# An attention step's fp32 products in two groups instead of three, tiles and scores alternating

## What is computed

```python
def _L0_attn_ref(hidden_states, Wq, Wkv, Wo):
    ...
    q = (hidden_states @ Wq).reshape(b, s, NUM_HEADS, HEAD_DIM)
    kv = hidden_states @ Wkv
    k, v = (kv[..., :HEAD_DIM], kv[..., HEAD_DIM:])
    scores = jnp.einsum('bqhd,bkd->bhqk', q, k) * scale
    bias = slopes[:, None, None] * (pos[None, None, :] - pos[None, :, None]).astype(jnp.float32)
    scores = jnp.where(causal[None, None], scores + bias[None], -jnp.inf)
    attn = jax.nn.softmax(scores, axis=-1)
    out = jnp.einsum('bhqk,bkd->bqhd', attn, v).reshape(b, s, h)
    return out @ Wo
...
x = x + _L0_attn_ref(_layernorm(x, axis=-1), Wq, Wkv, Wo)
x = x + _L0_ffn_ref(_layernorm(x, axis=-1), qweight, weight_scale, weight_zero_point, bias)
```

## Time and profile before

| | |
|---|---|
| median of three runs | 821.62 us (820.59 to 821.73) |
| the profiled execution | 822.31 us |
| its span, first to last instruction | 820.5 us |
| TensorE busy | 806.4 us (98%) |
| VectorE busy | 594.7 us (72%) |
| GpSimd busy | 429.4 us (52%) |
| ScalarE busy | 372.5 us (45%) |
| mean granted TensorE clock | 0.999 |

### The profile page before, as it was taken

The page is one execution under the profiler, slowest core; times in us unless marked ns, Lnnn a source line. Parts: engine busy times, 40 slices in busy tenths (PEclk is TensorE's granted clock), DMA queues, the critical chain, the costliest instruction groups (busy, mean ns, idle before and its releaser), DMA issues.

```text
span 820.5 us, 13647 instructions
## 1 busy us (share of the span) xinstructions
PE 806.4 (98%) x4618; PEld 583.2 (71%) x4618; DVE 594.7 (72%) x1589; ACT 372.5 (45%) x730; POOL 429.4 (52%) x313
## 2 busy tenths in 40 slices
PE   7999999999999999999999999999999999999997
PEld 5777878888665655556555555688887888888886
DVE  3877554577878889988888896255647779684877
ACT  1755536232466677676666665221401231051322
POOL 1000000000299998899889988522746298363566
PEclk9999999999999999999999999999999999999999
DMA  8867687467566655676566655462064613500012
GB/s 313 315 199 209 229 256 256 154 177 223 152 140 150 152 132 146 146 160 143 134 146 172 156 122 172 151 180 89 1 224 136 198 60 111 194 28 1 38 65 103
DMA packets 71390, 125.85 MB, mean 153 GB/s; under 512 B 7460, under 2 KB 16708, under 8 KB 71240
## 3 DMA queue, kind: packets, MB, share of 16 engines
q1 hardware_dynamic: 71312, 124.97, 52.5%
q10 hardware_dynamic: 8, 0.01, 0.0%
HBM read 85.61 MB, written 38.94 MB: 152 GB/s over the span
## 4 chain that ended last, share of the span: by engine, by line
PE 77%; DMA 7%; DVE 6%; issue 4%; ACT 4%; POOL 1%; SPq 0%; DVEq 0%; POOLq 0%; ACTq 0%
PE p_s L870 11%; PE p_st L899 9%; PE p_o L910 9%; PE p_s L978 5%; PE p_s L980 5%; PE p_s L979 5%; PE p_o L923 5%; PE p_o L809 4%; DMA inv_b<-inv_d 3%; PE p_s L809 2%; PE p_st L978 2%; PE p_st L980 2%; PE p_st L979 2%; PE p_s L1003 2%; PE p_s L1002 2%
## 5 line engine op out<-in xcount | busy, mean ns | idle before, releaser
L1452 DVE CUSTOM_DVE_ANT_0 spill<-p_s,mask 128x128 bf16<-128x128 f32 (+3 forms) x512 | 219.6, 483 | 38.3 <-PE p_s L870 37.6
L1169 ACT ACTIVATE pt<-p_st 128x512 f32<-128x512 f32 (+1 forms) x352 | 178.2, 562 | 101.1 <-PE p_st L899 100.9
L635 POOL TENSOR_SCALAR_AFFINE_SELECT pt<-pt 128x512 f32<-128x512 f32 x128 | 87.5, 696 | 238.7 <-ACT pt L1169 238.7
L870 PE MATMUL p_s<-kst,xt 98*128 98x128 f32 (+3 forms) x512 | 151.1, 343 | 0.9 <-DVE mx L1452 0.7
L899 PE MATMUL p_st<-xt,kst 100*128 100x512 f32 (+1 forms) x352 | 129.4, 387 | 0.7 <-DMA xt<-ml 0.3
L870 PEld LDWEIGHTS p_s<-kst,xt 98*128 98x128 f32 x512 | 91.4, 189 | 52.7 <-DVE mx L1452 42.7
L642 POOL TENSOR_TENSOR pt<-pt 128x1536 f32<-128x1536 f32 x32 | 111.8, 3492 | 2.7
L910 PE MATMUL p_o<-pt,vst 128*32 128x512 f32 (+3 forms) x1024 | 82.4, 439 | 0.0
L648 POOL TENSOR_TENSOR pt<-pt 128x1024 f32<-128x1024 f32 x32 | 76.7, 2396 | 0.0
L899 PEld LDWEIGHTS p_st<-xt,kst 100*128 100x128 f32 x352 | 64.5, 190 | 14.1 <-issue 5.6
L809 PE MATMUL p_o<-xt,wqh 128*128 128x512 f32 x136 | 53.1, 400 | 0.8 <-DVE xt L1603 0.8
(11 more groups left out here) (205 smaller groups left out, 1648.0 us busy)
## 6 DMA issues: line engine op xcount, KB each, us to landing
xt<-qh_d SPq DMA_DIRECT2D x64, 256.0 KB
xs<-in_x_t_dram SPq DMA_DIRECT2D x32, 256.0 KB, 6.2
qh_d<-qh SPq DMA_DIRECT2D x32, 256.0 KB, 3.2
ql_d<-ql SPq DMA_DIRECT2D x32, 256.0 KB, 4.1
xt<-ql_d SPq DMA_DIRECT2D x32, 256.0 KB
o_d<-o_st SPq DMA_DIRECT2D x32, 256.0 KB, 2.3
ob<-o_d SPq DMA_DIRECT2D x32, 256.0 KB, 5.5
xin<-in_x_dram SPq DMA_DIRECT2D x14, 512.0 KB, 7.8
```

The costliest lines, as they stand in the source:

```text
L635: pool.affine_select(out=own, in_=own, compare_op=ALU.is_ge, fill=0.0, base=0, pattern=[[0, 4], [1, P]], channel_multiplier=-1).then_inc(c ...
L870: pe.matmul(scores_of(n), qst[s % 4][0:R_MAX, j, qb * P:(qb + 1) * P], kst[0:R_MAX, b * S:b * S + keys], start=True, stop=True).then_inc(s ...
L1169: act.activation(pt[s % 2][:, j:j + heads, PT_AT[kb]:PT_AT[kb] + KB_LEN[kb]], p_st[:, place(k) % 3, 0:heads * KB_LEN[kb]].rearrange("p (j ...
L1452: dve.tensor_tensor_reduce(spill[:, SPILL_AT[qb]:SPILL_AT[qb] + keys], scores_of(n), mask[:, S - keys:S], 1.0, LOWEST, ALU.add, ALU.max, m ...
```

## The change

It rewrites the two tables of TensorE's order; the other engines' programs, the last step's groups behind the loop and `FIRST_AT` stay as they are.

```diff
-            ORDER = "xuxuxTGxuxuxuxuGuxuxxuuxGxu"
-
-            GROUP = (((0,), ()), ((1, 2, 3), ()), ((), (0, 1)))
+            ORDER = "xuxuxTGuxuxuxuxuxGuxuxuxux"
+
+            GROUP = (((0, 1), ()), ((2, 3), (0, 1)))
```

## The result

The changed kernel takes 840.61 us (median of 4 runs, 839.59 to 841.57) against 821.54 for the kernel before, a ratio of 1.0234 with a 95% interval of 1.0217 to 1.0252. It is slower by 19.1 us. The forecast was 841.9, with +20.3.

A forecast was written before the change was run, and what follows sets the result against it. TensorE was taken to bound the kernel before, at 9.38 us a step. The change's terms sum to +20.3 on the 820.5 us span; the profiled 822.31 becomes 842.6, and the median, 0.69 lower, 841.9 us, range 835 to 851.

The forecast's parts named there:

- U7 of step 1: Start of step 1's eighth score unit, after the wait for step 0's second add: 231.16 instead of 229.78, +1.38 us.
- 28 periods: Steps from U7 of step 1 to U7 of step 29: 28 x 10.15 against 263.89, +20.31 us.
- step 30: Period where VectorE's subtractions hold up GpSimd's cuts: 11.03 against 10.68, +0.35 us.
- step 31: Period that the output projection's first tiles fill on TensorE, longer than the ring: -0.30 us.
- behind U7 of step 31: After the last step's U7, step 30's sums and their entry and exit no longer stand: -1.40 us.
- The group saved: One fp32 group fewer per step on TensorE: 0.30 us saved, its own period from 9.38 to 9.08.
- The ring: Loop from U7 through GpSimd's second add and the sums back to U7: 10.15 us against TensorE's 9.08.
- The handoff: From GpSimd's second add's end to TensorE's sums: 0.14 us, bounds 0.05 to 0.30.
- It will idle 1.07 us in front of the sums.: TensorE, needing 9.08 us alone, waits 1.07 us for GpSimd's second add each step; the step grows 0.73 to 0.77.
- The rival with VectorE falling behind: In the steps, VectorE or the maxima's way falls behind the 1.07 us slack: 0.3 us each, 851; chance 0.06.
- The rival in which the ring does not bind: In the steps, only the group is saved: 821.6 - 9.3 = 812.3 us; chance 0.06.
- VectorE and GpSimd's port: VectorE's subtraction costs nothing; rival: some 26 get in front of an add, 0.6 us each, 858; chance 0.04.

The follow-up runs named there:

- with VectorE relieved and no ring: Changed kernel with its second group moved behind U9 and the maxima taken over the last 128 keys alone: 811.95 us.
- those with three: Kernel before the change, with the maxima taken over the last 128 keys alone: 816.79 us.
- longer by the values: Changed kernel with the sums put in front of the values of blocks 2 and 3 inside the second group: 858.25 us.
- with the ring shortened: Changed kernel with GpSimd's cuts of key blocks 2 and 3 over 8 columns of each head instead of 128: 835.21 us.
- The same order with short maxima: Changed kernel with the sums as a third group directly behind U7 and maxima over the last 128 keys alone: 842.72 us.
- The version with small cuts and short maxima: Changed kernel with cuts of blocks 2 and 3 over 8 columns of each head and maxima over the last 128 keys alone: 827.67 us.
- the changed kernel with short maxima: Changed kernel with VectorE's maxima over the last 128 keys alone instead of up to 512: 839.95 us.

## Why the prediction was right, and where it was not

| step of the forecast | forecast | measured |
|---|---|---|
| ring: U7 to the second add's end | 8.80 | 8.78 |
| ring: GpSimd's end to the sums | 0.14 | 0.06 |
| ring: the sums | 1.21 | 1.21 |
| U7 of step 1 | +1.38 | 230.86 - 229.78 = +1.08 |
| 28 periods | +20.31 | 283.82 - 263.89 = +19.93 |
| step 30 | +0.35 | 11.01 - 10.68 = +0.33 |
| step 31 | -0.30 | 12.41 - 13.17 = -0.76 |
| behind U7 of step 31 | -1.40 | (839.8 - 538.1) - (820.5 - 517.52) = -1.28 |
| sum | +20.3 | +19.3 of the span |

*The group saved.* Right in size: with VectorE relieved and no ring, the plain steps with two groups run at 8.95 us where those with three run at 9.27 (0.32, for a forecast of 0.30). That is the order with the second group behind U9, and over the 28 periods, late steps included, the two differ by only 0.13 (9.18 and 9.31). In the changed kernel none of it is seen.

*The ring.* Right, and shown from both sides: longer by the values (+0.65), longer by a GpSimd operation (+0.58), shortened or cut and the plain step falls.

*The handoff.* The term was 0.08 too long, some 2 us over the kernel. Other bounds added nearly as much: 283.82 is 2.4 more than 28 x 10.05, from the steps with reciprocals and from single steps, above all two (10.89, 10.62) in which TensorE waited for a transfer, 0.81 us for queries and 0.59 for maxima. So the agreement within 1.3 us owes something to two errors of opposite sign.

*"It will idle 1.07 us in front of the sums."* Wrong: 0.18 in a plain step, nothing in those with reciprocals. This part of the forecast's mechanism failed, and with it "TensorE's own period falls from 9.38 to 9.08" as what is left under the ring and, on VectorE, "so I take nothing here"; ScalarE's chain was not looked at. TensorE's path from U7 to the sums depends on both: with the ring shortened it takes 9.83 (10.12 with reciprocals), 9.67 when VectorE is relieved, 9.70 in the steps without the cast and the low part. The signs that the forecast named say so too. Its sums were to wait about 29 times, some 1 us each; they waited 12 times, 3.4 us in all. PE's share was to fall to about 95%; the page has 98%. Nor was TensorE to wait elsewhere in the step, and it did. U7 to the second add's end, the lengths of the adds and a steady period of about 10.1 came as named. The rival with VectorE falling behind was half true: its price of 0.3 us in every step came out as 0.07, only where the reciprocals stand. The total came out right because the ring hid these bounds, which lie 0.2 to 0.4 us under it; for the ring shortened by 0.8 us the same reasoning gave 812 to 822, and 835 was measured. The rival in which the ring does not bind (812.3) had a wrong number: with the ring shortened the same order runs at 835.

*VectorE and GpSimd's port.* No add was held up: the second adds are 2.38 and 2.40 long, none of the recorded ones over 2.41. VectorE's subtraction came 0.14 us before the add's end, and the cut of block 0 took 1.12 in place of 0.64, which cost the ring nothing, as forecast.

*The clock* stayed at 1.00 in all windows of the attention, in spite of the pauses; that rival found no support in the changed kernel.

## What to carry to other kernels

When a wait is moved ahead of an instruction, follow what that instruction feeds: if the awaited result depends on it one round later, the two close a ring, whose period is the sum of its parts however idle each engine looks, and an engine that is 90% busy may cost nothing while a 2.4 us operation decides. Before counting on the slack that a faster order leaves, add up every path that returns to the same engine: here the ring (10.05), what VectorE and ScalarE leave together (9.83) and what ScalarE leaves alone (9.67) stood within 4%, and removing the first alone gave 5 or 6 of the 19 us back. Long groups of one kind save switches, but starve an engine that lives on the other kind and can be fed only a few items ahead.

## What the runs showed of the hardware that was not expected

From the end of GpSimd's add to the start of TensorE's product that waited for it passed 0.06 us (287.48 + 2.40 to 289.94), less than the 0.14 behind VectorE's read the earlier trace rows.

In the version with the sums behind U7, step 24 took 14.9 us. TensorE waited there once for a transfer of queries, and the granted clock fell before the products went on (timeline of PE, then windows: length; PE, PEld, DVE, ACT, POOL busy; clock, DMA):

```profile
460.22 0.80 PE L870 MATMUL p_s<-kst,xt 98*128 98x128 f32 x2 [2.02 <-DMA xt<-ext_d]
...
462.79 3.21 PE L910 MATMUL p_o<-pt,vst 128*32 128x512 f32 x16
```

```profile
456.00:460.00 4.00, 2.20 (x20) 1.38 (x12) 2.35 (x10) 2.06 (x4) 3.92 (x3) 0.95 0.67 143
460.00:464.00 4.00, 3.78 (x15) 2.23 (x19) 2.10 (x9) 1.46 (x3) 3.45 (x3) 0.50 0.95 197
464.00:468.00 4.00, 3.88 (x21) 1.69 (x13) 0.79 (x5) 1.33 (x3) 0.17 (x1) 0.70 0.41 105
468.00:472.00 4.00, 4.00 (x41) 2.30 (x42) 2.79 (x12) 1.51 (x5) 1.72 (x3) 1.00 0.15 45
```

The values of blocks 0 and 1, 16 products, took 3.21 us at a granted 0.50 (1.2 GHz) instead of 1.71. The pauses of some tenths of a microsecond in every step of every version went with a granted 1.00. Between the two the traces show both. The same order with short maxima had pauses of 1.13, 2.02 and 1.06 us, each followed by a lower clock (windows of 4 us around them at 0.65, 0.77 and 0.82). The version with small cuts and short maxima had a pause of 1.18 us that left the clock at 1.00 and one of 1.14 us with a lower clock (windows around them):

```profile
440.00:444.00 4.00, 2.96 (x25) 1.72 (x17) 1.75 (x13) 2.56 (x6) 2.66 (x3) 1.00 0.78 194
472.00:476.00 4.00, 2.86 (x13) 1.67 (x15) 2.08 (x16) 2.69 (x6) 4.00 (x4) 0.75 0.70 125
```

In the changed kernel with short maxima a pause of 1.45 us left it at 1.00 as well. So the length of one pause does not tell whether the clock falls; what does, and why the queries were late in those steps, was not tried.
